# A recommendation tower: all pair dots of a tile in one piece, with layers 1 and 2 in another shape, layer 3 on VectorE and the table lookups in another order

## The chip, the cores and the metric

The kernel runs on one core of a Trainium2 chip. The metric is the time on the device in microseconds (us), as a median of runs; lower is better.

## The reference, cut to what matters

For each of 2048 rows of a batch, 27 embedding rows of 128 floats are looked up, one in each of 27 tables, by integer ids. The dot products of all 351 pairs of the 27 rows follow, 16 dense values are appended, and three dense layers end in one number for each row.

```python
e = jnp.stack([tbl_f[ids[:, f]] for f in range(27)], axis=1)   # (2048, 27, 128)
dot = jnp.einsum('bnd,bmd->bnm', e, e)                         # all pairs
z = flat[:, idx]                                               # the 351 pairs i < j
h = jnp.concatenate([z, dense_ctx], axis=1)                    # (2048, 367)
h = jnp.maximum(h @ W_top1 + b_top1, 0.0)                      # (2048, 512)
h = jnp.maximum(h @ W_top2 + b_top2, 0.0)                      # (2048, 256)
y = h @ W_top3                                                 # (2048, 1)
```

## The kernel before, in words

**Tiles.** The batch is cut into 16 tiles of 128 rows. Two neighbouring tiles make a half (`HT = 2`, 8 halves of 256 rows). Everything is float32.

**Two ways to look up.** 17 features are gathered (`GATHERED`): GpSimd issues one indirect DMA for each feature and tile (L298), 272 in all, into `emb`, which holds two tiles; a slot is free again once TensorE has turned the rows of two tiles ago. TensorE transposes them four features at a time, a "quad" (L331; five quads to a tile, the last with one feature), and ScalarE copies each quad into `embT` (L488). The ten smallest tables (`ONE_HOT`, seven of 1000 rows and three of 1250) stay in SBUF, split into two parts. VectorE compares the broadcast ids of a half with row numbers and so builds one-hot matrices (L426), one for each chunk of 125 table rows, 8 or 10 chunks to a table; TensorE multiplies both parts of the chunk with it, 256 columns wide (L321); ScalarE copies the result (L481). One such step for a half and a table is a "hot" step, 80 in all. The one-hot matrices live in `SLOTS` = 6 groups of two chunks, and VectorE builds one table ahead (`LOOK = 1`). SyncE loads the ids of a table `IDS` tables ahead (L247), in its queue behind the tables and the weights.

**Dots.** For each batch row TensorE multiplies the 27 columns of `embT` with themselves (L347), 128 such products to a tile. They come as 256 pairs of a weight load and a matmul of 27 columns each, so 512 instructions to a tile. The four 32-partition strips of `gram_ps` take four rows at a time. VectorE then transposes the result into `flat` (L442, L443) and ScalarE copies each pair once into `pairs` (L496, the step "ring").

**Layers.** "flat" turns `pairs` (three transposes, L359) and copies them to `flatT` (L500). Layer 1 is 12 matmuls, 128 wide (24 matmul instructions, L370), then a ReLU on ScalarE (L505); layer 2 is 8 matmuls (16 instructions, L380), then bias and ReLU in two halves (L513); layer 3 is 2 matmuls with a single weight column (4 instructions, L387) and a copy (L521).

**Order.** `plan(t)` writes the steps of tile t down by hand (L93 to L125) and `ORDER` is run through in the same order by TensorE, ScalarE and VectorE. After `START`, with the ten hot steps of half 0 between the quads of tile 0, come four hot steps of half 1. From then on an odd tile t carries: its five quads; the dots of tile t-1 in four pieces of 8 groups (64 instruction pairs), one behind each of the first four quads; flat, layer 1, layer 2 and layer 3 of tile t-2, one behind each of these pieces; and the last six hot steps of the next half. An even tile has its dots in three pieces (80, 88 and 88 pairs) with nothing but a quad and a layer between them, and all its four hot steps at its end. The dots of a tile wait for its last quad and for the last hot step of its own half; in the order before, that step is over a whole tile earlier. SyncE stores two tiles of results at a time from one partition (L236).

Of the kernel before, what the change touches and what calls it, by code (L numbers as in the profile page):

```python
# [43 lines left out]
def dlrm_tower(nc, dense, idx_rows, ids_hot, tables, w1, w2, b2, w3, y):  # L44
# [4 lines left out]
    C2 = w3.shape[1]  # L49
    H2 = C2 * P  # L50
# [15 lines left out]
    PITCH = 28  # L66
# [7 lines left out]
    IDS = 7  # L74
# [6 lines left out]
    YB = 2  # L81
# [10 lines left out]

    def plan(t):  # L93
        h, odd = divmod(t, HT)
        last = t == T - 1
        hots = []
        if h + 1 < HALVES:
            first = O * 2 // 5
            hots = [("hot", h + 1, o) for o in (range(first, O) if odd else range(first))]
        parts = 2 if last else 4 if odd else 3  # L100
        dots = []
        if t > 0:
            cuts = [GROUPS32 * i // parts for i in range(parts + 1)]
            dots = [("dots", t - 1, a, b) for a, b in zip(cuts, cuts[1:])]
        rest = [(kind, t - 2) for kind in ("flat", "layer1", "layer2", "layer3")] if t > 1 else []
        held = 0 if odd else QUADS - 2
        out = []
        for q in range(QUADS):
            if t > 0:
                out.append(("quad", t, q))  # L110
            out += dots[q:q + 1]
            if last and q == 1:
                out += rest[1:]
            elif last and q == 2:
                out += [("ring", t - 1), ("flat", t - 1)]
            elif last and q == 3:
                out += [(kind, t - 1) for kind in ("layer1", "layer2", "layer3")]
            elif not last or q == 0:
                out += rest[q:q + 1]
            if q >= held:  # L120
                a, b = q - held, QUADS - held
                out += hots[len(hots) * a // b:len(hots) * (a + 1) // b]
        if t > 0 and not last:
            out.append(("ring", t - 1))
        return out  # L125

    HOT0 = [("hot", 0, o) for o in range(O)]
    START = []
    for q in range(QUADS):
        START += HOT0[O * q // QUADS:O * (q + 1) // QUADS] + [("quad", 0, q)]  # L130
    END = [("dots", T - 1, 0, GROUPS32), ("ring", T - 1)]
    END += [(kind, T - 1) for kind in ("flat", "layer1", "layer2", "layer3")]
    ORDER = START + [step for t in range(T) for step in plan(t)] + END

# [10 lines left out]
    with ctx:  # L145
# [20 lines left out]
        flatT = sb("flatT", [P, 2, KC, TILE])  # L166
        h1T = sb("h1T", [P, C1, TILE])
        h2T = sb("h2T", [P, C2, TILE])
        y_sb = sb("y_sb", [1, 2, YB * TILE])
        w1_sb = sb("w1_sb", [P, KC, H1])  # L170
        w2_sb = sb("w2_sb", [P, C1, H2])
        w3_sb = sb("w3_sb", [P, C2])
        b2_sb = sb("b2_sb", [P, C2])
# [13 lines left out]
        out_ps = ps("out_ps", [P, 512])  # L187
# [18 lines left out]
        staged = [sem(f"staged{o}") for o in range(O)]  # L206
        high_ready = sem("high_ready")
# [19 lines left out]
        y_summed = sem("y_summed")  # L227
        y_ready = sem("y_ready")
        y_stored = [sem(f"y_stored{b}") for b in range(2)]
# [4 lines left out]
        def store(sp, b):  # L234
            sp.wait_ge(y_ready, YB * (b + 1))
            sp.dma_start(y[b * YB * TILE:(b + 1) * YB * TILE, :].rearrange("n a -> a n"),  # L236
                         y_sb[0:1, b % 2, :]).then_inc(y_stored[b % 2], 16)

        @block.sync
        def _(sp):  # L240
# [24 lines left out]
            sp.dma_start(w3_sb[:, :], w3).then_inc(weights_loaded, 16)  # L265
            sp.dma_start(b2_sb[:, :], b2).then_inc(weights_loaded, 16)  # L266
            stored = 0
            for n in range(O, len(HOTS)):

                if HOTS[n][1] - 1 >= stored + 3:  # L270
                    store(sp, stored)
                    stored += 1
                load_ids(n)
            for b in range(stored, T // YB):
                store(sp, b)
            for b in range(2):
                sp.wait_ge(y_stored[b], 16 * (T // YB // 2))

# [25 lines left out]
        def _(pe):  # L304
# [57 lines left out]
            def layer1(t):  # L362
                pe.wait_ge(flatT_ready, t + 1)
                if t == 0:
                    pe.wait_ge(weights_loaded, WEIGHTS)
                else:
                    pe.wait_ge(h1_ready, t)
                for c in range(C1):
                    for k in range(KC):
                        mm = pe.matmul(h1_ps[:, c * TILE:(c + 1) * TILE], w1_sb[0:KR, k, c * P:(c + 1) * P],  # L370
                                       flatT[0:KR, t % 2, k, :], start=(k == 0), stop=(k == KC - 1))
                mm.then_inc(h1_summed, 1)

            def layer2(t):
                pe.wait_ge(h1_ready, t + 1)
                if t > 0:
                    pe.wait_ge(y_ready, t)
                for c in range(C2):
                    for k in range(C1):
                        mm = pe.matmul(out_ps[:, c * TILE:(c + 1) * TILE], w2_sb[:, k, c * P:(c + 1) * P],  # L380
                                       h1T[:, k, :], start=(k == 0), stop=(k == C1 - 1))
                mm.then_inc(h2_summed, 1)

            def layer3(t):
                pe.wait_ge(h2_ready, C2 * (t + 1))
                for k in range(C2):
# [188 lines left out]
```

## Time and profile before

| | |
|---|---|
| median of 3 runs | 405.42 us (403.98 to 406.58) |
| the profiled execution | 406.24 us, of which the span from first to last instruction is 404.4 us |
| TensorE (PE) matmuls busy | 362.8 us, 90% |
| TensorE weight loads (PEld) | 331.7 us, 82% |
| VectorE (DVE) | 253.3 us, 63% |
| ScalarE (ACT) | 170.9 us, 42% |
| GpSimd (POOL) | 260.9 us, 65% |
| mean granted TensorE clock | 0.975 of full |

The profile is one execution. "Idle before" is the time that an engine stood still ahead of a group of instructions, with what released it; "issue" there means that nothing in the profile shows what it waited for. SPq is SyncE's queue. Matmuls overlap in the pipeline, so the time that one group costs is read from its start to the start of the next one.

### The profile page before, as it was taken

How to read it: one execution, taken by the hardware profiler on the slowest of the kernel's cores; microseconds unless marked ns; L12 is line 12 of the kernel's file. 1: busy time of each engine (PE TensorE's matmuls, PEld its weight loads, DVE VectorE, ACT ScalarE, POOL GpSimd, SP SyncE). 2: the span in 40 equal slices, each digit the busy share in tenths (PEclk: the TensorE clock that was granted, in tenths of full speed). 3: DMA queues.
4: the chain of work that ended last, by engine and by line, in shares of the span. 5: the costliest groups of instructions: out<-in, count | busy, mean ns of one | idle time of the engine just before them, and what ended most of it. 6: DMA issues, size and time to landing. Idle time of an engine off the chain costs nothing.

```text
span 404.4 us, 14846 instructions
## 1 busy us (share of the span) xinstructions
PE 362.8 (90%) x6496; PEld 331.7 (82%) x6496; DVE 253.3 (63%) x751; ACT 170.9 (42%) x267; POOL 260.9 (65%) x280
## 2 busy tenths in 40 slices
PE   1887699999998999999998999999998999986846
PEld 1766599889997999989997999899988999865745
DVE  4999799939665684929583866749492966311010
ACT  3455325354534354354334454535334454463311
POOL 6777777777777777777777777777777777100000
PEclk9998989999999999999999999999999999999877
DMA  6999985343333242323433243324333322000000
GB/s 184 234 239 228 220 133 120 82 86 89 88 76 94 61 106 73 89 72 95 93 79 88 69 107 77 89 61 107 81 83 78 80 55 55 23 3 3 0 3 0
DMA packets 23233, 36.44 MB, mean 90 GB/s; under 512 B 6425, under 2 KB 17441, under 8 KB 23169
## 3 DMA queue, kind: packets, MB, share of 16 engines
q1 hardware_dynamic: 14464, 17.66, 18.9%
q0 software_dynamic: 8704, 17.84, 18.8%
q8 instruction: 51, 0.84, 0.8%
q14 instruction: 14, 0.11, 0.1%
HBM read 35.47 MB, written 0.01 MB: 88 GB/s over the span
## 4 chain that ended last, share of the span: by engine, by line
PE 79%; DMA 5%; ACT 4%; DVE 4%; issue 4%; SPq 3%; DVEq 0%; ACTq 0%
PE embT_ps L321 39%; PE h_ps L370 12%; PE gram_ps L347 11%; PE out_ps L380 8%; PE embT_ps L331 5%; DMA ids<-in_ids_hot 4%; DVE one_hot L426 3%; PE flat_ps L359 2%; PE out_ps L387 2%; SPq L265 2%; ACT pairs L496 1%; ACT h2T L513 1%; DVE tbl L412 1%; DMA embT<-in_tbl 1%; SPq L266 1%
## 5 line engine op out<-in xcount | busy, mean ns | idle before, releaser
L298 POOL DMA_INDIRECT emb<-in_tbl,idx x272 | 260.0, 956 | 84.2 <-issue 81.5
L426 DVE TENSOR_SCALAR one_hot<-ids,row_of 125x256 fp32r<-125x256 int32 x688 | 214.8, 386 | 43.2 <-PE embT_ps L321 40.5
L321 PE MATMUL embT_ps<-one_hot,tbl 125*128 125x256 f32 x1376 | 192.4, 294 | 19.0 <-DVE one_hot L426 18.8
L321 PEld LDWEIGHTS embT_ps<-one_hot,tbl 125*128 125x128 f32 x1376 | 175.9, 195 | 31.2 <-issue 15.9
L481 ACT COPY embT<-embT_ps 128x256 f32<-128x256 f32 x80 | 53.0, 662 | 131.0 <-PE embT_ps L321 131.0
L488 ACT COPY embT<-embT_ps 128x512 f32<-128x512 f32 (+1 forms) x80 | 81.9, 1024 | 0.6 <-PE embT_ps L331 0.5
L442 DVE STREAM_TRANSPOSE flat<-gram_ps 128x864 f32<-128x864 f32 x16 | 17.3, 1083 | 87.9 <-PE gram_ps L347 87.9
L347 PEld LDWEIGHTS gram_ps<-embT 128*27 128x27 f32 x4096 | 42.7, 104 | 18.0 <-issue 14.9
L347 PE MATMUL gram_ps<-embT 128*27 128x27 f32 x4096 | 50.8, 193 | 6.8 <-issue 5.7
L370 PE MATMUL h_ps<-flatT,w_sb 126*128 126x128 f32 x384 | 51.2, 294 | 1.9 <-issue 1.1
L370 PEld LDWEIGHTS h_ps<-flatT,w_sb 126*128 126x128 f32 x384 | 48.1, 206 | 3.1 <-ACT flatT L500 1.3
L331 PE MATMUL embT_ps<-ident,emb 128*128 128x128 f32 x272 | 43.3, 275 | 0.0
L380 PE MATMUL out_ps<-h1T,w_sb 128*128 128x128 f32 x256 | 32.9, 282 | 2.1 <-ACT h1T L505 2.1
L331 PEld LDWEIGHTS embT_ps<-ident,emb 128*128 128x128 f32 x272 | 32.4, 142 | 0.7 <-issue 0.7
L380 PEld LDWEIGHTS out_ps<-h1T,w_sb 128*128 128x128 f32 x256 | 29.8, 191 | 3.2 <-ACT h1T L505 2.7
L505 ACT ACTIVATE h1T<-h_ps 128x512 f32<-128x512 f32 x16 | 9.6, 599 | 50.6 <-PE h_ps L370 50.6
L513 ACT ACTIVATE h2T<-out_ps,b_sb 128x128 f32<-128x128 f32 x32 | 10.0, 364 | 28.2 <-PE out_ps L380 28.2
L412 DVE TENSOR_TENSOR tbl<-embT,tbl 125x1024 fp32r<-125x1024 f32 (+1 forms) x10 | 13.3, 1327 | 5.3 <-ACT tbl L469 5.3
L496 ACT COPY pairs<-flat 128x351 f32<-128x351 f32 x16 | 13.3, 830 | 6.3 <-DVE flat L443 6.3
L469 ACT CAST tbl<-embT 125x1024 fp32r<-125x1024 f32 (+1 forms) x10 | 11.2, 1115 | 10.7 <-DMA embT<-in_tbl 10.7
L359 PE MATMUL flat_ps<-ident,pairs 128*126 128x128 f32 x48 | 9.1, 300 | 5.9 <-ACT pairs L496 5.3
L387 PE MATMUL out_ps<-h2T,w_sb 128*1 128x128 f32 x64 | 9.6, 271 | 4.1 <-ACT h2T L513 4.1
(18 smaller groups left out, 37.9 us busy)
## 6 DMA issues: line engine op xcount, KB each, us to landing
ids<-in_ids_hot SPq DMA_DIRECT2D x80, 128.0 KB
emb<-in_tbl,idx POOLq DMA_INDIRECT x272
embT<-in_tbl SPq DMA_DIRECT2D x7, 448.0 KB
embT<-in_tbl SPq DMA_DIRECT2D x3, 560.0 KB
w_sb<-in_W_ring SPq DMA_DIRECT2D x1, 756.0 KB
w_sb<-in_W_top SPq DMA_DIRECT2D x1, 512.0 KB
embT<-in_tbl SPq DMA_DIRECT2D x7, 52.0 KB
idx<-in_idx_rows SPq DMA_DIRECT2D x1, 202.5 KB, 7.9
```

What stands on the lines that cost most here:

```text
L298: pool.indirect_dma_start(emb[:, t % EB, s, :], None, tables[f][:, :], bass.IndirectOffsetOnAxis(ap=idx[:, t, f:f + 1], axis=0),).then_inc ...
L321: mm = pe.matmul(out[:, 0:HN], tbl[0:ROWS, part, AT[o] + chunk, :], one_hot[0:ROWS, k % SLOTS, c, :], start=(chunk == 0 and part == 0), st ...
L331: mm = pe.transpose(out[:, i * P:(i + 1) * P], emb[:, t % EB, s, :], ident[:, :])
L347: mm = pe.matmul(gram_ps[32 * j:32 * j + FEATS, b, at * FEATS:(at + 1) * FEATS], rows, rows, start=True, stop=True)
L370: mm = pe.matmul(h1_ps[:, c * TILE:(c + 1) * TILE], w1_sb[0:KR, k, c * P:(c + 1) * P], flatT[0:KR, t % 2, k, :], start=(k == 0), stop=(k = ...
L380: mm = pe.matmul(out_ps[:, c * TILE:(c + 1) * TILE], w2_sb[:, k, c * P:(c + 1) * P], h1T[:, k, :], start=(k == 0), stop=(k == C1 - 1))
L387: mm = pe.matmul(out_ps[0:1, C2 * TILE:(C2 + 1) * TILE], w3_sb[:, k:k + 1], h2T[:, k, :], start=(k == 0), stop=(k == C2 - 1))
L412: dve.tensor_tensor(tbl[0:ROWS, 1, AT[o]:AT[o + 1], :], raw(o, 0, ROWS).rearrange("p (c d) -> p c d", d=D), tbl[0:ROWS, 0, AT[o]:AT[o + 1] ...
L426: done = dve.tensor_scalar(one_hot[0:ROWS, k % SLOTS, c, :], ids[0:ROWS, n % IDS, :], row_of[0:ROWS, KINDS.index(CH[o]), chunk:chunk + 1], ...
L481: act.copy(embT_feats[:, at:at + HT, GF + o, :], embT_ps[USE["hot", h, o] % BANKS][:, 0:HN].rearrange("p (t c) -> p t c", t=HT),).then_inc ...
L488: act.copy(embT_feats[:, t % TB, quad(q)[0]:quad(q)[0] + n, :], embT_ps[USE["quad", t, q] % BANKS][:, 0:n * P].rearrange("p (f c) -> p f c ...
L496: act.copy(pairs[:, t % 2, :, 1:HALF + 1], ring()).then_inc(pairs_ready, 1)
```

## The change

- The dots of tile t-1 stand in one piece behind the first quad of tile t (`cuts = [0, GROUPS32]`).
- The hot steps are spread evenly: five in each tile, one behind each quad. Half h is looked up in the tiles 2h-1 and 2h, so its last hot step is the last step but one ahead of the first quad of tile 2h+1, behind which the dots of tile 2h stand. The four hot steps of half 1 ahead of tile 1 are gone from there.
- Layer 1 runs for two tiles at once, 256 columns wide, in two calls of 6 matmuls in the odd tiles; layer 2 swaps its operands (`h1T` is the weight, `w2` moves with 256 columns), 4 matmuls to a tile, two tiles in the even tiles. The last two tiles run layer 1 alone.
- Layer 3 leaves TensorE and ScalarE: VectorE adds the bias (from PSUM) and then multiplies, clamps and sums in one instruction. `w3` and `b2` are broadcast over the partitions when loaded, and each tile's result is stored by itself, a number to a partition.
- For half 0 ScalarE turns the ids into floats before VectorE reads them. `PITCH`, the row pitch of `embT`, goes from 28 to 27 floats, `IDS` from 7 to 6.

```diff
-    PITCH = 28
+    PITCH = FEATS
-    IDS = 7
+    IDS = 6
     def plan(t):
-        h, odd = divmod(t, HT)
+        h, odd = divmod(t + 1, HT)
+        odd = 1 - odd
...
+        if t == 0:
+            hots = HOT0
+        elif h < HALVES:
+            hots = [("hot", h, o) for o in (range(O // 2) if odd else range(O // 2, O))]
+        cuts = [0, GROUPS32]
+        dots = [("dots", t - 1, a, b) for a, b in zip(cuts, cuts[1:])] if t > 0 else []
+        after = [[] for _ in range(QUADS)]
+        if t > 1:
+            after[0].append(("flat", t - 2))
+        if t > 2 and odd:
+            after[1].append(("layer1", t - 3))
+            after[2].append(("layer1", t - 2))
+        elif t > 2:
+            after[1].append(("layer2", t - 4))
+            after[2].append(("layer2", t - 3))
+        if t == T - 1:
+            after[3] += [("layer2", t - 3), ("ring", t - 1), ("flat", t - 1), ("layer2", t - 2)]
         out = []
         for q in range(QUADS):
+            mine = hots[len(hots) * q // QUADS:len(hots) * (q + 1) // QUADS]
+            if t == 0:
+                out += mine
+            out.append(("quad", t, q))
+            out += dots[q:q + 1]
+            out += after[q]
             if t > 0:
+                out += mine
+        if 0 < t < T - 1:
             out.append(("ring", t - 1))
...
+    END = [("dots", T - 1, 0, GROUPS32), ("layer1", T - 2), ("ring", T - 1), ("flat", T - 1), ("layer2", T - 2),
+           ("layer1", T - 1), ("layer2", T - 1)]
...
+            def layer1(n):
+                alone = n >= T - HT
...
+                width = TILE if alone else HT * TILE
+                first, count = (0, C1) if alone else (n % HT * C1 // HT, C1 // HT)
+                for i in range(count):
+                    c = first + i
                     for k in range(KC):
+                        mm = pe.matmul(h1_ps[:, i * width:(i + 1) * width], w1_sb[0:KR, k, c * P:(c + 1) * P],
+                                       x[:, k, :], start=(k == 0), stop=(k == KC - 1))
...
+                for k in range(C1):
+                    mm = pe.matmul(h2_ps[:, :], h1T[:, k, t % HT * TILE:(t % HT + 1) * TILE], w2_sb[:, k, :],
+                                   start=(k == 0), stop=(k == C1 - 1))
...
+            def layer3(t):
+                dve.wait_ge(h2_summed, t + 1)
...
+                dve.tensor_tensor(h2[:, :], h2_ps[:, :], b2_sb[:, :], ALU.add).then_inc(h2_ready, 1)
+                dve.wait_ge(h2_ready, t + 1)
+                dve.scalar_tensor_tensor(h2[:, :], h2[:, :], 0.0, w3_sb[:, :], ALU.max, ALU.mult,
+                                         accum_out=y_sb[:, t:t + 1]).then_inc(y_ready, 1)
...
+            def float_ids(n):
+                act.wait_ge(ids_loaded[n % IDS], 16 * (n // IDS + 1))
+                act.copy(ids[0:ROWS, n % IDS, :].bitcast(F32), ids[0:ROWS, n % IDS, :]).then_inc(ids_as_floats, 1)
```

## Rows read from the trace of the kernel before

**Rows 1.** The page: TensorE clock and DMA rate in 40 equal slices; the chain by line.

```profile
PEclk9998989999999999999999999999999999999877
...
GB/s 184 234 239 228 220 133 120 82 86 89 88 76 94 61 106 73 89 72 95 93 79 88 69 107 77 89 61 107 81 83 78 80 55 55 23 3 3 0 3 0
...
PE embT_ps L321 39%; PE h_ps L370 12%; PE gram_ps L347 11%; PE out_ps L380 8%; PE embT_ps L331 5%; DMA ids<-in_ids_hot 4%; DVE one_hot L426 3%; PE flat_ps L359 2%; PE out_ps L387 2%; SPq L265 2%; ACT pairs L496 1%; ACT h2T L513 1%; DVE tbl L412 1%; DMA embT<-in_tbl 1%; SPq L266 1%
```

**Rows 2.** Groups of TensorE from 99.6 to 358.7 us, the tiles 3 to 14.

```profile
L347 PE MATMUL gram_ps<-embT 128*27 128x27 f32 x3072 | 38.8, 192 | 2.5 <-issue 2.1
...
L387 PE MATMUL out_ps<-h2T,w_sb 128*1 128x128 f32 x48 | 7.2, 271 | 1.7 <-ACT h2T L513 1.7
```

**Rows 3.** Timeline of TensorE in tile 7: start us, us, what.

```profile
194.34 2.94 PE L370 MATMUL h_ps<-flatT,w_sb 126*128 126x128 f32 x24
197.04 2.17 PE L321 MATMUL embT_ps<-one_hot,tbl 125*128 125x256 f32 x16
199.04 0.60 PE L331 MATMUL embT_ps<-ident,emb 128*128 128x128 f32 x4
199.58 0.74 PE L347 MATMUL gram_ps<-embT 128*27 128x27 f32 x64
200.25 2.05 PE L380 MATMUL out_ps<-h1T,w_sb 128*128 128x128 f32 x16
202.06 2.16 PE L321 MATMUL embT_ps<-one_hot,tbl 125*128 125x256 f32 x16
```

**Rows 4.** Timeline of TensorE: the second of three pieces of dots in tile 8.

```profile
216.29 1.09 PE L347 MATMUL gram_ps<-embT 128*27 128x27 f32 x76
218.42 0.30 PE L347 MATMUL gram_ps<-embT 128*27 128x27 f32 x12 [1.04 <-issue]
```

**Rows 5.** Timeline of TensorE in tile 15 and behind it.

```profile
358.77 0.77 PE L331 MATMUL embT_ps<-ident,emb 128*128 128x128 f32 x5
...
363.86 0.93 PE L347 MATMUL gram_ps<-embT 128*27 128x27 f32 x87 [1.62 <-issue]
...
375.15 4.55 PE L370 MATMUL h_ps<-flatT,w_sb 126*128 126x128 f32 x24
...
384.49 1.80 PE L347 MATMUL gram_ps<-embT 128*27 128x27 f32 x193 [0.48 <-ACT embT L488]
388.28 0.78 PE L347 MATMUL gram_ps<-embT 128*27 128x27 f32 x63 [1.99 <-issue]
...
393.01 5.49 PE L370 MATMUL h_ps<-flatT,w_sb 126*128 126x128 f32 x24 [0.57 <-ACT flatT L500]
```

**Rows 6.** Stretches: from:to, length, busy of PE, PEld, DVE, ACT, POOL, granted clock, DMA.

```profile
361.70:365.10 3.40, 1.78 (x132) 1.65 (x132) 0.27 (x1) 1.21 (x2) 0.00 (x0) 1.00 0.03 5
...
385.60:389.00 3.40, 1.41 (x146) 1.23 (x133) 0.00 (x0) 0.00 (x0) 0.00 (x0) 0.97 0.02 5
389.00:399.20 10.20, 6.46 (x32) 5.70 (x28) 1.64 (x3) 1.86 (x3) 0.00 (x0) 0.51 0.01 2
```

**Rows 7.** DMA queues: TensorE's instructions as they are fetched (packets, MB).

```profile
q8 instruction: 51, 0.84, 0.8%
```

**Rows 8.** Timeline of the start: TensorE and VectorE around the first ids of half 1.

```profile
47.77 0.27 PE L331 MATMUL embT_ps<-ident,emb 128*128 128x128 f32 x1
...
49.83 12.35 DVE L426 TENSOR_SCALAR one_hot<-ids,row_of 125x256 fp32r<-125x256 int32 x40 [2.69 <-DMA ids<-in_ids_hot]
```

**Rows 9.** Timeline: TensorE at tile 3, then ScalarE, VectorE and GpSimd in the loop.

```profile
99.60 0.60 PE L331 MATMUL embT_ps<-ident,emb 128*128 128x128 f32 x4
...
278.37 0.66 ACT L481 COPY embT<-embT_ps 128x256 f32<-128x256 f32 x1 [1.24 <-PE embT_ps L321]
...
205.38 1.08 DVE L442 STREAM_TRANSPOSE flat<-gram_ps 128x864 f32<-128x864 f32 x1 [0.70 <-PE gram_ps L347]
...
206.97 8.70 DVE L426 TENSOR_SCALAR one_hot<-ids,row_of 125x256 fp32r<-125x256 int32 x28
...
344.95 0.94 POOL L298 DMA_INDIRECT emb<-in_tbl,idx  x1 [0.31 <-issue]
```

More of the change, by code:

```diff
@@ L48, in dlrm_tower @@
     KR, KC, H1 = w1.shape
-    C2 = w3.shape[1]
-    H2 = C2 * P
+    H2 = w2.shape[1]
     C1 = H1 // P
@@ L93, in plan @@
     def plan(t):
-        h, odd = divmod(t, HT)
-        last = t == T - 1
+        h, odd = divmod(t + 1, HT)
+        odd = 1 - odd
         hots = []
[L97 to L104, printed above, removed]
@@ L105, in plan @@
-        rest = [(kind, t - 2) for kind in ("flat", "layer1", "layer2", "layer3")] if t > 1 else []
-        held = 0 if odd else QUADS - 2
+        if t == 0:
[7 more added lines that the diff above has]
+            after[0].append(("flat", t - 2))
@@ L112, in plan @@
[L112 to L122, printed above, removed]
@@ L127, in dlrm_tower @@
     HOT0 = [("hot", 0, o) for o in range(O)]
[L128 to L133, printed above, removed]
+    END = [("dots", T - 1, 0, GROUPS32), ("layer1", T - 2), ("ring", T - 1), ("flat", T - 1), ("layer2", T - 2),
+           ("layer1", T - 1), ("layer2", T - 1)]
+    ORDER = [step for t in range(T) for step in plan(t)] + END
     USE = {step: u for u, step in enumerate(step for step in ORDER if step[0] in ("quad", "hot"))}
@@ L226, in dlrm_tower, with halves_of, store @@
         h2_ready = sem("h2_ready")
-        y_summed = sem("y_summed")
         y_ready = sem("y_ready")
-        y_stored = [sem(f"y_stored{b}") for b in range(2)]
+        y_stored = sem("y_stored")
         WEIGHTS = 16 * 4
         block = ctx.enter_context(nc.Block())
[L234 to L237, printed above, removed]
+        def halves_of(t):
+            return t if t >= T - HT else t // HT * HT + HT - 1
+        def store(sp, t):
+            sp.wait_ge(y_ready, t + 1)
+            sp.dma_start(y[t * TILE:(t + 1) * TILE, :], y_sb[:, t:t + 1]).then_inc(y_stored, 16)
         @block.sync
@@ L273, in _ @@
                 load_ids(n)
[L274 to L277, printed above, removed]
+            for t in range(stored, T):
+                store(sp, t)
+            sp.wait_ge(y_stored, 16 * T)
         @block.gpsimd
@@ L376, in layer2 @@
                 if t > 0:
[L377 to L381, printed above, removed]
-                mm.then_inc(h2_summed, 1)
-            def layer3(t):
-                pe.wait_ge(h2_ready, C2 * (t + 1))
-                for k in range(C2):
-                    mm = pe.matmul(out_ps[0:1, C2 * TILE:(C2 + 1) * TILE], w3_sb[:, k:k + 1], h2T[:, k, :],
-                                   start=(k == 0), stop=(k == C2 - 1))
-                mm.then_inc(y_summed, 1)
+                    pe.wait_ge(h2_ready, t)
@@ L418, in build @@
                 _, _, o = HOTS[n]
-                dve.wait_ge(ids_loaded[n % IDS], 16 * (n // IDS + 1))
+                of = ids[0:ROWS, n % IDS, :]
+                if n < O:
+                    dve.wait_ge(ids_as_floats, n + 1)
+                    of = of.bitcast(F32)
+                else:
+                    dve.wait_ge(ids_loaded[n % IDS], 16 * (n // IDS + 1))
                 for i in range(GROUPS[o]):
@@ L425, in build @@
                         chunk = i * GROUP + c
-                        done = dve.tensor_scalar(one_hot[0:ROWS, k % SLOTS, c, :], ids[0:ROWS, n % IDS, :],
+                        done = dve.tensor_scalar(one_hot[0:ROWS, k % SLOTS, c, :], of,
                                                  row_of[0:ROWS, KINDS.index(CH[o]), chunk:chunk + 1], None,
@@ L528, in _ @@
                     split_high(ahead)
+                    float_ids(ahead)
                     ahead += 1
```

83 lines of the change are left out of this document (35 added, 48 removed).

## The prediction, made before the changed kernel was run

> **What bounds the kernel now.** The chain of waits comes first: nearly 80% of it is TensorE work, half of that the one-hot products of L321 [rows 1]. TensorE bounds the kernel, and between tile 3 and tile 15 it hardly stands still. So a step is priced by what it takes from TensorE, start to start. In tile 7 [rows 3]: layer 1 takes 197.04 - 194.34 = 2.70 us (24 instructions, 112 ns each); a hot step of 8 chunks 2.00 us, or 0.25 us a chunk; a quad 0.54; 64 pairs of the dots 0.67 (10.5 ns a pair); layer 2 1.81. VectorE needs 8.70 / 28 = 0.311 us for a chunk and 1.59 us for the two transposes and the dense columns behind the dots [rows 9]. GpSimd issues its last gather at 344.95 us [rows 9], nearly 40 us ahead of the last quad, so it stays off the path unless TensorE gains more than that.
>
> The second view is where TensorE waits for "issue". It does so inside long runs of dots and nowhere else in the loop: 1.04 us behind 76 pairs in tile 8 [rows 4], 1.62 us in tile 15, and 1.99 us in the one place where 256 pairs already stand in one piece, behind the loop [rows 5]. There 193 pairs run for 1.80 us, TensorE idles 1.99, and 63 more take 0.78: 4.57 us for work that at 10.5 ns a pair takes 2.7. The queue that brings TensorE's instructions moved 0.84 MB in 51 packets [rows 7]; 6496 weight loads and as many matmuls are 12992 instructions, so a packet holds about 255 of them, 128 pairs. My reading, an estimate: dots eat a packet in 1.3 us, the next is asked for when the one before it is begun, and it is usable 3.1 to 3.7 us later. 3.4 - 1.3 = 2.1 us of standstill for each piece of 256 pairs. Of the Trainium skill, "Runtime: NRT & Kernel Launch", section "Instruction fetch mechanics", says the opposite: the fetch is hidden, because dispatch is slower than the refill. The trace disagrees, with 1.99 us. By the page there would be no standstill; that is a rival below.
>
> The third view is the clock. It is full through the loop [rows 1]. Behind the burst with 1.62 us of idle it stayed full (361.7 to 365.1 us, 1.00); behind the one with 1.99 us it fell to its lower level, 1.2 GHz: 389.0 to 399.2 us at 0.51 [rows 6], where layer 1 took 5.49 us instead of 2.9 [rows 5].
>
> **The parts, against the span of 404.4 us.** The profiled execution took 406.24 us, 1.84 more than its span and 0.8 more than the median.
>
> *To quad (3,0), before at 99.60 us [rows 9].* The last quad of tile 0 starts at 47.77 us, and the first ids of half 1 let VectorE build on at 49.83, after 2.69 us of idle [rows 8]. Now a quad and dots stand there, and the wait is covered. `w3` and `b2` as broadcasts put 0.26 MB ahead of these ids, about 1.1 us at the 220 to 239 GB/s of those slices [rows 1]; that is covered too, all but some 1 us where VectorE's transposes queue behind the late build. Floats instead of integers could speed up VectorE's first 86 chunks, but the tables' landing paces them as well: 0, bounds -1.5 and +1. So quad (1,0) at 48.0; tile 1 costs 0.54 + 4.7 (dots) + 10.0 (five hot steps) + 1.7 (the other 13 transposes) + 1 = 17.9; tile 2 costs 0.54 + 4.7 + 0.4 (flat) + 11.5 (46 chunks) + 1.7 + 0.35 = 19.2. That ends at 85.1, 14.5 us earlier, but four hot steps (8.0 us) and the layers of tile 0 are still to do.
>
> *Tiles 3 to 14, before 259.2 us (99.60 to 358.77) [rows 9, 5].* Plus 8.0 for the four hot steps. Dots: 12 pieces of 4.7 us against 38.8 + 2.5 us [rows 2]: +15.1. Layer 3: 7.2 + 1.7 us go, less the overlap of its matmuls' ends: -8.2 [rows 2]. Layer 1 has half the instructions, each twice as wide; no row has the shape. It could cost no more than a narrow one (112 ns, a gain of 2.7 us a pair of tiles) or twice as much; since a 27-column pair takes 10.5 ns and a 128-column instruction 112, columns count, and I take twice. The same for layer 2, 8 x 0.224 = 1.79 against 1.81. Both: -1. The flat transposes no longer wait for the ring: -1.1. The dots of even tiles now wait for the copy of the hot step just ahead (0.66 us [rows 9], of which a quad hides most): 6 x 0.35 = +2.1. VectorE's order matters, since it waits for the dots and for each layer 2 before it builds on: behind dots it has one table in stock (2.0 us of TensorE) plus flat and a quad (0.94), and needs 1.59 + 0.62 for the next group; its two instructions for layer 3 have no row, 0.3 to 0.5 us each by the 0.311 of a chunk, and in 22 us it has some 6 idle. I take 0. ScalarE's added and removed work, single-tile stores and `IDS` 6 lie beside other work: 0; if ids came late, VectorE would starve. `PITCH` 27: 0, bounds 10% of the dots each way, 4 us. Sum: 259.2 + 8.0 + 15.1 - 8.2 - 1 - 1.1 + 2.1 = 274.1, so quad (15,0) at 359.2, level with before.
>
> *Tail, before 45.6 us.* Now, in order: quad and wait 0.9, dots 4.7, flat 0.4, three quads 1.6, two double layer 1 calls 5.4, two layer 2 3.6, flat 0.4, waits for ReLUs 0.5, last quad 0.13 and its copy 0.6, dots 4.6, layer 1 of tile 14 2.7 (which hides transposes and ring), flat 0.4, layer 2 1.8, layer 1 2.7, ReLU 0.7, layer 2 1.8, VectorE 0.9, store 1.6: 35.4, or 10 less. It saves the lone waits of four small layers and the low clock in layer 1 (4.55 and 5.49 us [rows 5]). End 394.6.
>
> *Where packets end.* A tile has about 775 instructions, three packets and a few, so the ends of packets drift slowly through the dots. Near their head or tail a second standstill comes. By my count this meets tiles 12 to 15; bounds 1 and 8 us, taken 4. 398.6.
>
> *The clock.* Every piece now has the idle behind which the clock fell once. The fall depends on where the idle lies, so I take it for 7 of 16 pieces. A short low stretch costs 4.55 - 2.9 = 1.7 us [rows 5], so 12 us: span 410.6, time 412.4, and by the median 411.6.
>
> **Rivals.**
> *A, the clock holds.* The standstill is below what matters, as at 1.62 us. Decides if it stays near 1.8 us. Place: behind each piece of dots; price 12 us less. Time 399.6, faster. For it: one burst with 1.62 us, full clock. Against: 1.99 us and a fall, on the same form. Chance 0.22, give or take 5 us.
> *B, short standstills.* The fetch is asked for earlier in the loop than behind it, and costs 1.0 us as in tile 8: 16 x 1.1 less and no falls, no second ones: about 378; up to 391 in between. Against it: tile 8 reached 1.04 us with a quad and a flat between. Chance 0.14.
> *C, no standstill.* 34 us less than the 394.6, but gathers end at 346 and the rest of the tail takes 22: 368 to 370. The Trainium skill's "Runtime: NRT & Kernel Launch" would have it so. The rows contradict it: 0.03.
> *D, long falls.* Each fall lasts 10 us as behind the loop, with 5 us lost: 398.6 + 36 + 1 = 435. For it, the one row there is; against, layer 1 at 375.15 ran low for one stretch only. Chance 0.11.
>
> **How the numbers follow.** My forecast has 0.50, its own range 405 to 421 (4 to 10 falls, packets, pitch). The 8-in-10 range leaves out D, C and the better half of B: 389 to 422. A measurement of this kernel tells 1% from no change, so faster means below 401.4 and slower above 409.5. Faster: B, C and 0.13 of A, 0.30. Within: 0.09 of A and 0.15 of the forecast, 0.24. Slower: 0.46.
>
> **What will show it.** In the changed profile: in each tile one group of about 185 to 200 pairs of L347, an idle of 1.9 to 2.2 us put down to "issue", then the rest; L347's idle sum near 32 us. The granted clock below full in slices of the loop, with hot steps of 4 us instead of 2.0. Quad (3,0) near 85 us, quad (15,0) between 359 and 372. The gap in front of the dots of even tiles near 0.35 us, no VectorE waits above it. L370 with half the instructions at 220 ns. I am wrong if the dots run through, if VectorE starves TensorE behind them, or if the wide matmuls cost as little as narrow ones (-20 us).

## The result: slower by 9.5%, outside the range

| | before | changed |
|---|---|---|
| median of 4 runs each, on one chip | 404.82 us (403.98 to 406.58) | 443.68 us (441.0 to 446.71) |
| ratio | | 1.0953 (95%: 1.0897 to 1.1009) |
| the profiled execution | 406.24 us, span 404.4 | 444.45 us, span 441.3 |
| mean granted clock | 0.975 | 0.921 |

Slower had the largest chance, but the time lies 21.7 us above the upper end of the range. On another chip the changed kernel took 437.65 us against 407.79, a ratio of 1.0743. So its price is 30 to 39 us.

The page of the changed kernel, against [rows 1]: busy time by engine, the clock in 40 slices, the DMA queue that SyncE's transfers are in (packets, MB, share of 16 engines), and the chain by engine.

```profile
span 441.3 us, 14146 instructions
PE 361.4 (82%) x6136; PEld 333.0 (75%) x6136; DVE 261.5 (59%) x799; ACT 167.6 (38%) x229; POOL 264.9 (60%) x280
...
PEclk9999869998989898999889896999969998997987
...
q1 hardware_dynamic: 16752, 17.92, 17.3%
...
PE 75%; issue 12%; DMA 7%; ACT 3%; DVE 1%; POOL 1%; SPq 0%; ACTq 0%; DVEq 0%
```

TensorE has 5% fewer instructions and is busy for as long as before. What grew is the time in which it waits for nothing that the profile shows: "issue" is 12% of the chain, 53 us (4% before). And the clock is now below full in slices all through the loop.

The groups of TensorE in tiles 3 to 14 (93.25 to 391.4 us), against [rows 2]:

```profile
L346 PE MATMUL gram_ps<-embT 128*27 128x27 f32 x3072 | 50.6, 205 | 32.4 <-issue 26.9 <-ACT embT L499 2.2
...
L375 PE MATMUL h_ps<-flatT,w_sb 126*128 126x256 f32 x144 | 33.1, 379 | 0.0
L384 PE MATMUL h_ps<-w_sb,h1T 128*128 128x256 f32 x96 | 22.7, 379 | 0.0
```

The dots cost 50.6 + 32.4 = 83.0 us in twelve tiles, 6.9 a piece, where 4.7 were forecast and 3.4 was the price before.

Two kinds of pieces make this up. They are named by the tile in whose steps they stand (it is the dots of the tile before). First the timeline of TensorE in tile 11, which stands for the odd tiles:

```profile
292.24 1.98 PE L346 MATMUL gram_ps<-embT 128*27 128x27 f32 x146 [0.38 <-ACT embT L499]
296.18 1.76 PE L346 MATMUL gram_ps<-embT 128*27 128x27 f32 x110 [1.96 <-issue]
```

That is the forecast's picture: one standstill of 1.96 us in the middle, where by the forecast's count a packet of instructions ends. In the tiles 3, 4, 5, 7, 9, 11 and 13 it comes after 186, 183, 176, 166, 156, 146 and 136 pairs: the end of the packet drifts by ten pairs in two tiles. Now tile 10, which stands for the tiles 6, 8, 10, 12 and 14, and SyncE's queue just ahead of it:

```profile
264.40 1.08 PE L346 MATMUL gram_ps<-embT 128*27 128x27 f32 x78
268.15 0.23 PE L346 MATMUL gram_ps<-embT 128*27 128x27 f32 x2 [2.67 <-issue]
268.97 0.18 PE L346 MATMUL gram_ps<-embT 128*27 128x27 f32 x1 [0.60 <-issue]
...
270.21 3.77 PE L346 MATMUL gram_ps<-embT 128*27 128x27 f32 x174 [0.42 <-issue]
```

```profile
259.80 0.91 SPq L237 DMA_DIRECT2D out_y<-y_sb  x2
```

TensorE stops after 78 pairs, then does a pair or two at a time with 0.4 to 0.6 us between them, then runs on at the lower clock: 9.5 us for a piece. Some 5.5 us before the stop SyncE issued two stores of `y`. It issues one at 160.24 us, two at 208.80, 259.80 and 311.20 and three at 361.77, and the dots stop at 165.6, 214.5, 265.5, 316.5 and 367.5, after 60 to 93 pairs. That is ahead of the place where a packet ends in the tiles beside them (176 to 136 pairs). The pieces of the tiles 6, 8, 10, 12 and 14 take 9.23, 8.52, 9.52, 8.77 and 7.11 us, those of the odd tiles between them 4.8 to 5.7. Each store writes 128 single numbers from 128 partitions: the queue q1 has 16752 packets where a kernel with a single store at the end (below) has 14480, 142 more for each of the 16.

Stretches of the changed kernel (from:to, length, busy of PE, PEld, DVE, ACT, POOL, granted clock, DMA), behind the dots of tile 10 and of tile 11 and over the loop:

```profile
264.00:269.00 5.00, 1.71 (x86) 1.40 (x84) 0.42 (x2) 2.33 (x3) 3.78 (x5) 1.00 0.83 58
269.10:275.80 6.70, 5.58 (x185) 4.93 (x185) 1.77 (x4) 0.48 (x1) 2.57 (x3) 0.50 0.28 75
...
296.40:299.70 3.30, 3.30 (x116) 3.17 (x103) 1.72 (x4) 0.48 (x1) 2.01 (x3) 0.50 0.18 46
...
64.00:391.00 327.00, 291.48 (x5030) 271.88 (x5029) 208.40 (x664) 129.57 (x176) 216.85 (x226) 0.93 0.37 73
```

Behind a stop the granted clock is 0.50, that is 1.2 GHz. Over the loop it is 0.93, so TensorE is at 1.2 GHz for some 14% of 327 us, 45 us in ten stretches, and loses up to 22 us by it.

### The profile page after: what moved, and what is told of

Same layout as the page of the kernel before. It is cut to its first block, busy times and chain, and to the rows that moved or that the text cites. A ratio compares the mean times of both kernels' runs of the same rounds, so it can differ in the third digit from the quotient of the medians.

```text
span 441.3 us, 14146 instructions
## 1 busy us (share of the span) xinstructions
PE 361.4 (82%) x6136; PEld 333.0 (75%) x6136; DVE 261.5 (59%) x799; ACT 167.6 (38%) x229; POOL 264.9 (60%) x280
## 3 DMA queue, kind: packets, MB, share of 16 engines
q1 hardware_dynamic: 16752, 17.92, 17.3%
## 4 chain that ended last, share of the span: by engine, by line
PE 75%; issue 12%; DMA 7%; ACT 3%; DVE 1%; POOL 1%; SPq 0%; ACTq 0%; DVEq 0%
PE embT_ps L320 36%; PE gram_ps L346 14%; PE h_ps L375 10%; PE h_ps L384 6%; PE embT_ps L330 6%; DMA embT<-in_tbl 4%; PE flat_ps L358 2%; DMA emb<-in_tbl,idx 2%; ACT embT L499 1%; POOL emb L297 1%; DVE one_hot L426 1%; ACT tbl L483 0%; ACT embT L506 0%; DMA idx<-in_idx_rows 0%; DVE tbl L407 0%
## 5 line engine op out<-in xcount | busy, mean ns | idle before, releaser
L426 DVE TENSOR_SCALAR one_hot<-ids,row_of 125x256 fp32r<-125x256 int32 (+1 forms) x688 | 210.5, 380 | 30.2 <-PE embT_ps L320 24.9
L320 PE MATMUL embT_ps<-one_hot,tbl 125*128 125x256 f32 x1376 | 202.1, 303 | 19.7 <-DVE one_hot L426 18.0
L320 PEld LDWEIGHTS embT_ps<-one_hot,tbl 125*128 125x128 f32 x1376 | 185.6, 203 | 25.9 <-issue 15.4
L346 PE MATMUL gram_ps<-embT 128*27 128x27 f32 x4096 | 64.0, 204 | 47.9 <-issue 40.8
L346 PEld LDWEIGHTS gram_ps<-embT 128*27 128x27 f32 x4096 | 52.5, 115 | 60.8 <-issue 52.6
L375 PE MATMUL h_ps<-flatT,w_sb 126*128 126x256 f32 (+1 forms) x216 | 46.5, 369 | 0.3 <-ACT h1T L528 0.3
L375 PEld LDWEIGHTS h_ps<-flatT,w_sb 126*128 126x128 f32 x216 | 38.2, 202 | 4.6 <-issue 0.5
L518 ACT COPY flatT<-flat_ps 126x384 f32<-126x384 f32 x16 | 7.7, 480 | 79.4 <-PE flat_ps L358 79.4
L384 PE MATMUL h_ps<-w_sb,h1T 128*128 128x256 f32 x128 | 30.6, 382 | 1.2 <-ACT h1T L524 0.7
L384 PEld LDWEIGHTS h_ps<-w_sb,h1T 128*128 128x128 f32 x128 | 23.1, 190 | 4.3 <-ACT h1T L524 0.9
L528 ACT ACTIVATE h1T<-h_ps 128x512 f32<-128x512 f32 x14 | 8.4, 598 | 19.5 <-PE h_ps L375 19.5
L483 ACT CAST tbl<-embT 125x1024 fp32r<-125x1024 f32 (+1 forms) x10 | 11.3, 1132 | 10.7 <-DMA embT<-in_tbl 10.7
```

The source lines that it names most:

```text
L320: mm = pe.matmul(out[:, 0:HN], tbl[0:ROWS, part, AT[o] + chunk, :], one_hot[0:ROWS, k % SLOTS, c, :], start=(chunk == 0 and part == 0), st ...
L346: mm = pe.matmul(gram_ps[32 * j:32 * j + FEATS, b, at * FEATS:(at + 1) * FEATS], rows, rows, start=True, stop=True)
L375: mm = pe.matmul(h1_ps[:, i * width:(i + 1) * width], w1_sb[0:KR, k, c * P:(c + 1) * P], x[:, k, :], start=(k == 0), stop=(k == KC - 1))
L384: mm = pe.matmul(h2_ps[:, :], h1T[:, k, t % HT * TILE:(t % HT + 1) * TILE], w2_sb[:, k, :], start=(k == 0), stop=(k == C1 - 1))
L426: done = dve.tensor_scalar(one_hot[0:ROWS, k % SLOTS, c, :], of, row_of[0:ROWS, KINDS.index(CH[o]), chunk:chunk + 1], None, ALU.is_equal)
```

## The experiments

The theory on record, **packets**: a piece of 256 pairs eats instructions faster than they are fetched, and the standstills let the clock fall. Its rival, found in the timeline, **stores**: the stores of single numbers slow the supply of instructions down when dots stand behind them, and so make longer standstills and more falls.

### Each alone and both

*Four pieces.* The dots of a tile in four pieces of 64 pairs, one behind each quad:

```diff
-        cuts = [0, GROUPS32]
+        cuts = [GROUPS32 * i // 4 for i in range(5)]
```

> The changed kernel with the dots of a tile in four pieces again, one behind each of the first four quads; all else stays. Theory: the loss is the one piece, that is the standstills of TensorE inside it and the clock falls behind them. Then the dots of a tile cost 3.0 to 3.4 us instead of the 6.7 us measured in tiles 3 to 14, the clock stays full in the loop, and the time falls to 370 to 392 us, under the kernel before. Rival: the new table order or the layers cost as much as the one piece, VectorE starving TensorE; then it stays above 410 us with DVE waits on L320.

*One store.* All results are kept, turned by TensorE at the end and stored by one DMA of 16 rows:

```diff
-                while HT * HOTS[n][1] - 1 >= stored + 7:
-                    store(sp, stored)
-                    stored += 1
                 load_ids(n)
-            for t in range(stored, T):
-                store(sp, t)
-            sp.wait_ge(y_stored, 16 * T)
+            sp.wait_ge(y_copied, 1)
+            sp.dma_start(y.rearrange("(t p) a -> t (p a)", p=TILE), y_rows[:, :]).then_inc(y_stored, 16)
+            sp.wait_ge(y_stored, 16)
...
+            pe.wait_ge(y_ready, T)
+            pe.transpose(flat_ps[0:T, 0:P], y_sb[:, :], ident[:, :]).then_inc(y_turned, 1)
```

> The changed kernel, dots in one piece, but the results are kept in SBUF, turned once at the end and stored by one DMA of 16 rows, in place of 16 stores of 128 single numbers. Theory S: these stores disturb TensorE's instruction supply; the standstills of 7 to 9.5 us in tiles 6, 8, 10, 12 and 14 go, each of these blocks takes about 5 us like the odd ones, and the time falls by 18 to 25 us to 418 to 426 us. Rival P: they come from where the instruction packets end in the dots; then the blocks stay at 7 to 9.5 us and the time stays within 4 us of 443.7.

*Both edits.*

> Both of the above: four pieces and one store. Theory S: a little below the kernel with four pieces alone, by 2 to 10 us, since its supply is disturbed less: 365 to 385 us. Rival P: the same as with four pieces alone, within 2 us.

*The kernel before, its dots in one piece*, without anything else of the change:

```diff
-        parts = 2 if last else 4 if odd else 3
+        parts = 1
```

> The kernel before with one thing changed: the dots of a tile in one piece behind its first quad. It has no small stores. My mechanism (a standstill of 1.1 to 2.3 us in each piece, then a clock fall behind most of them): dots 5.0 us a tile instead of 3.4, plus 8 to 12 low stretches of 1.7 us, so 425 to 445 us. Rival: the piece costs little where hot steps follow densely and the clock holds: 405 to 415 us.

The kernel before took 407.42 us beside them. The upper left number is the changed kernel's, from other chips. Of the four runs of one piece with one store, one took 402.95 us at a mean clock of 0.979 and three took 409.6 to 410.2 at 0.958 to 0.967, so it has no ratio:

| | 16 small stores | one store |
|---|---|---|
| one piece | 443.7 (437.7 on a third chip) | 409.71 (402.95 to 410.24) |
| four pieces | 402.98, ratio 0.9851 (0.981 to 0.9892) | 387.92, ratio 0.9541 (0.9491 to 0.959) |

The kernel before in one piece: 437.08 us, ratio 1.0765 (1.0713 to 1.0817), so 29.7 us more than with its pieces. Of the four expectations only this one was met. The two kernels with four pieces came out slower than expected, and one store in one piece faster.

Groups of dots over the whole run of these kernels, the first of four pieces, the second of one store (a run of 409.83 us), the third of both, the fourth of the kernel before in one piece:

```profile
L346 PE MATMUL gram_ps<-embT 128*27 128x27 f32 x4096 | 56.7, 193 | 10.5 <-issue 5.6 <-ACT embT L499 2.6 <-ACT embT L506 1.0
```

```profile
L341 PE MATMUL gram_ps<-embT 128*27 128x27 f32 x4096 | 54.5, 199 | 34.6 <-issue 27.6 <-ACT embT L496 2.6 <-ACT embT L503 1.0
```

```profile
L341 PE MATMUL gram_ps<-embT 128*27 128x27 f32 x4096 | 55.9, 193 | 7.0 <-issue 2.8 <-ACT embT L496 2.6 <-ACT embT L503 1.0
```

```profile
L347 PE MATMUL gram_ps<-embT 128*27 128x27 f32 x4096 | 54.0, 194 | 29.5 <-issue 25.0 <-ACT embT L488 0.5
```

Both causes are there, and they feed each other. A piece of 256 pairs stands still for 27.6 / 16 = 1.7 us and 25.0 / 16 = 1.6 us on average in the two kernels that have no small stores (single pieces 0.6 to 3.1 us); with four pieces 2.8 us are left in all. In the table, one piece costs 15.0 to 21.8 us with one store (by the run of 402.95 or by the median) and 35 to 41 with sixteen; sixteen stores cost 15.1 us with four pieces and 28 to 41 with one. With one piece and sixteen stores part of the width comes from comparing chips.

The stretches of the loop show the clock's part: one store with one piece, then with four (columns as above).

```profile
64.00:368.00 304.00, 276.51 (x4982) 258.86 (x4980) 205.29 (x647) 125.43 (x172) 212.96 (x224) 0.96 0.31 78
```

```profile
61.00:363.00 302.00, 295.75 (x5304) 266.30 (x5303) 210.56 (x656) 131.39 (x183) 215.79 (x228) 1.00 0.31 79
```

At 0.96 the loss is some 0.04 x 304 = 12 us, at 1.00 it is none. The last column but one is the DMA engines' busy share, 0.31 with one store. With sixteen it is 0.39 from 64 to 364 us, and the queues say where the rise lies (packets, MB, share of 16 engines): first the changed kernel, then one piece with one store, both from 64 to 364 us.

```profile
q0 software_dynamic: 7081, 14.53, 26.3%
q1 hardware_dynamic: 10224, 8.25, 11.2%
```

```profile
q0 software_dynamic: 7221, 14.80, 20.1%
q1 hardware_dynamic: 8830, 8.04, 10.2%
```

q1 holds the small stores, q0 GpSimd's gathers. The stores' own queue rises by one point only. The gathers rise by six, with fewer packets (27.9% against 19.6% with four pieces). So the small stores take little time of the engines themselves; it is the packets of another queue that take longer while the stores are under way. The instructions come as packets too, in q8. Here are the same queues of the changed kernel for 6 us each: from 264 us, with the stop of tile 10, and from 290.5 us, with the dots of tile 11.

```profile
q0 software_dynamic: 99, 0.20, 65.5%
...
q8 instruction: 1, 0.02, 3.9%
```

```profile
q0 software_dynamic: 157, 0.33, 21.8%
...
q8 instruction: 1, 0.02, 1.0%
```

3.9% of 16 engines over 6 us are 3.7 us for one packet of instructions, 1.0% are 1.0 us. The trace has each such packet with its start and length. Those of the tiles 10, 12 and 14 took 3.74, 3.30 and 2.49 us; those of the tiles 6 and 8 took 0.93 and 0.97 but started 3.8 and 4.6 us behind the first dots, against 0.95 to 2.1 us in the other tiles from 2 to 13. So in the five tiles with stores just ahead the packet had landed 3.2 to 5.6 us behind the first dots, in the others 2.0 to 3.1. With one store, in one piece, none took over 1.6 us in the whole run, though in tile 4 the packet landed 4.1 us behind the first dots and the piece idled 2.65. That the instructions come late behind small stores is shown by this; why the stores hold other packets up, and why TensorE stops ahead of the end of a packet, is not.

### A chip on which nothing could be told

Four kernels ran twice on a chip on which the kernel before itself took 678 us. Their granted clock was 0.79 to 0.82, and in the first of them TensorE idled for "issue" in the table steps too (23.7 us). The first is the changed kernel with its stores moved in SyncE's queue, to the ids of another table:

```diff
-                while HT * HOTS[n][1] - 1 >= stored + 7:
+                while HOTS[n][2] == 2 and HT * HOTS[n][1] - 1 >= stored + 7:
```

> Again the changed kernel with only the moment of the loop's small stores moved to just behind the dots of the even tiles, since on the chip of the run before the kernel before itself took 678 us. Theory S: the blocks of 7 to 9.5 us in the tiles 6, 8, 10 and 12 fall to 5 to 6 us; the time falls by 10 to 16 us against 443.7, so 1.05 to 1.07 times the kernel before. Rival, number of stores or SyncE's waits: 1.085 to 1.10 times.

The second has one store and the dots in two pieces, `cuts = [0, GROUPS32 // 2, GROUPS32]`:

> Again the kernel with one store and the dots in two pieces of 128 pairs. Packet theory: a packet of instructions is 128 pairs long, so the standstill in a piece is 0 to 0.7 us and the clock holds: 0.95 to 0.97 times the kernel before. Rival, each piece stands still by itself: 0.985 to 1.01 times.

The third is the kernel before in one piece, with sixteen stores of 128 numbers each in place of its eight stores of rows (the numbers stored are taken from `dense_sb`, so `y` is left out):

> Again the kernel before with dots in one piece (1.077 times the kernel before) and its 8 row stores replaced by 16 stores of 128 single numbers taken from the dense values (the output is not the result). Theory S: blocks of 7 us and more where a store comes shortly ahead of the dots; 1.09 to 1.13 times. Rival, small stores harmless here: 1.07 to 1.085 times.

The fourth has one store and multiplies only every second group of pairs, so half of the dots is left out:

> Again the kernel with one store and one piece, with every second group of the dots left out (128 pairs a tile, half of the dot products missing). Packet theory: no standstill over 0.5 us in most tiles, full clock in the loop, 365 to 385 us where the kernel before takes 405. Rival, the standstill belongs to the step: 1.5 us or more in most tiles.

| | first time | second time |
|---|---|---|
| kernel before | 678.13 | 679.11 |
| stores moved | 586.33 | 589.23, ratio 0.8654 (0.8553 to 0.8754) |
| two pieces, one store | 631.91 | 632.86, ratio 0.9286 |
| before, one piece, small stores | 626.98 | 618.28, ratio 0.9041 |
| half the dots (one run each) | 539.23 | 538.16 |

The dots of the kernel with its stores moved idled 110.4 us on that chip, 98.7 of it for "issue"; on a normal chip they idle 47.5 in all. Here the kernel with one piece beats the kernel before by 13% and two pieces by 7%, another order than on the normal chips. What slows this chip wasn't found, and these runs decide nothing about the theories. Half the dots never ran on a normal chip, so of short pieces only those of the kernel with two pieces were measured there.

### The same on a normal chip

The kernel before took 407.79 us here. First the changed kernel itself again:

> The changed kernel itself, unaltered, beside the three below on the same chip: 1.09 to 1.10 times the kernel before where that takes 405 us; where it takes 678 us, Theory S makes it slower than with the stores moved (0.865 times), the rival within 1% of that.

437.65 us, ratio 1.0743 (1.0651 to 1.0836), below the expected 1.09. Then with its stores moved (the edit above):

> The changed kernel with only the moment of the loop's small stores moved to just behind the dots of the even tiles. Theory S: the blocks of 7 to 9.5 us in the tiles 6, 8, 10, 12 fall to 5 to 6 us, 10 to 16 us less than the changed kernel beside it. Rival, number of stores or SyncE's waits: within 4 us of it.

438.88 us, ratio 1.0763 (1.0686 to 1.084): no gain, which is the rival's number. The timeline says why: a store in SyncE's queue, and TensorE around it.

```profile
259.71 1.77 SPq L237 DMA_DIRECT2D out_y<-y_sb  x2
```

```profile
259.18 2.34 PE L346 MATMUL gram_ps<-embT 128*27 128x27 f32 x153
...
265.83 0.25 PE L346 MATMUL gram_ps<-embT 128*27 128x27 f32 x3 [1.79 <-issue]
```

SyncE runs some steps ahead, and the stores went out during the dots instead of just ahead of them. The stop with single pairs behind it came later in the piece, after 249 pairs here, but it came. My expectation had put the stores in the wrong place.

The kernel before with one piece and small stores:

> The kernel before with dots in one piece (1.077 times the kernel before) and 16 stores of 128 single numbers, taken from the dense values, in place of 8 row stores (the output is not the result). Theory S: blocks of 7 us and more where a store comes shortly ahead of the dots, 1.09 to 1.13 times the kernel before. Rival, small stores harmless here: 1.07 to 1.085 times.

470.85 us, ratio 1.1567 (1.1483 to 1.165): 33.8 us more than in one piece with its own stores (437.08, on another chip). But for the one piece, nothing of the change is in this kernel. Its SyncE queue, its TensorE behind a store, and its dots over the whole run:

```profile
254.89 0.91 SPq L237 DMA_DIRECT2D out_y<-dense_sb  x2
```

```profile
258.38 1.11 PE L349 MATMUL gram_ps<-embT 128*27 128x27 f32 x104
263.74 0.54 PE L349 MATMUL gram_ps<-embT 128*27 128x27 f32 x2 [4.25 <-issue]
```

```profile
L349 PE MATMUL gram_ps<-embT 128*27 128x27 f32 x4096 | 60.0, 199 | 47.3 <-issue 42.3 <-ACT embT L490 0.5
```

The same stop, 4.25 us long, 4.6 us behind the store, then single pairs. "Issue" went from 25.0 to 42.3 us. So the small stores alone do it, in another order of steps and other layers, and for more than the expected 1.13. The moment isn't what differs: with its own stores of rows the same kernel issues five of them 3.4 to 3.6 us ahead of a piece, and these pieces take 4.6 to 5.8 us without single pairs. With small stores at the same distance they take 8.1 to 10.7. The form of the stores and their number (16 for 8) changed together, and no run tells these two apart.

Two pieces and one store:

> The kernel with one store and the dots in two pieces of 128 pairs. Packet theory: a packet of instructions is 128 pairs long, so the standstill in a piece is 0 to 0.7 us and the clock holds: 0.95 to 0.97 times the kernel before. Rival, each piece stands still by itself: 0.985 to 1.01 times.

390.34 us, ratio 0.9563 (0.9491 to 0.9636), about as much as four pieces. Its dots idle 7.4 us for "issue" in all.

A piece of 128 pairs, one packet, mostly runs through (25 of 30 in this run; the other five idle 0.3 to 1.6 us), and the clock doesn't fall from 65.7 to 373 us. That fits a piece being harmless as long as it is no longer than the instructions that lie ready; how many lie ready, no row says.

### Stores amid the table steps, and the best kernel

The stores moved again, by `HOTS[n][2] == 3`, so that they go out in the table steps, some 10 us behind the start of the dots in even tiles:

> The changed kernel (1.074 to 1.095 times the kernel before) with the loop's small stores moved once more: with two loads of ids they had gone out during the dots of the even tiles, now they go out some 10 us behind their start, 13 us ahead of the next dots. Theory S (a small store disturbs TensorE's instruction supply 3.4 to 9 us after it is issued): all blocks in the loop 5 to 6.5 us, 1.03 to 1.05 times the kernel before. Rival, the number of small stores counts and not their moment: 1.07 times or more.

431.01 us, ratio 1.0587 (1.0489 to 1.0684) beside 407.5 of the kernel before: between the two expectations, and its interval overlaps that of the unaltered changed kernel (1.0651 to 1.0836). So the time hardly decides, but the timeline does. TensorE's dots in tile 10, a store behind them, and the stretch behind the store:

```profile
255.06 2.60 PE L346 MATMUL gram_ps<-embT 128*27 128x27 f32 x153
258.88 1.47 PE L346 MATMUL gram_ps<-embT 128*27 128x27 f32 x103 [1.22 <-issue]
```

```profile
265.23 0.92 SPq L237 DMA_DIRECT2D out_y<-y_sb  x2
```

```profile
264.00:269.00 5.00, 5.00 (x35) 4.69 (x34) 4.64 (x17) 2.22 (x3) 3.85 (x4) 1.00 0.72 72
```

The DMA engines are nearly as busy as behind the store of the changed kernel (0.72, against 0.83 there), but TensorE runs through, 5.00 of 5.00 us: a table step takes 35 matmuls in that time, where dots would take over 200. The pieces of the tiles 2 to 13 take 4.3 to 6.7 us, none with single pairs. Yet the time is only 6.6 us less than on the chip above: three of the later stores go out together at 341.84 us, just ahead of tile 14, and two more around the last dots at 394.65. The piece in tile 14 takes 8.5 us and the last one 9.2.

At last the best parts together. Four pieces, one store, and the dots of the last tile in two pieces with layer 1 of tile 14 between them (the first two edits, and this):

```diff
-    END = [("dots", T - 1, 0, GROUPS32), ("layer1", T - 2), ("ring", T - 1), ("flat", T - 1), ("layer2", T - 2),
-           ("layer1", T - 1), ("layer2", T - 1)]
+    END = [("dots", T - 1, 0, GROUPS32 // 2), ("layer1", T - 2), ("dots", T - 1, GROUPS32 // 2, GROUPS32),
+           ("layer2", T - 2), ("ring", T - 1), ("flat", T - 1), ("layer1", T - 1), ("layer2", T - 1)]
```

> The kernel with four pieces and one store (0.954 times the kernel before), and the last tile's dots, which still stood in one piece at the end (5.4 us with a standstill of 2.8), in two pieces with layer 1 of tile 14 between and layer 2 of tile 14 behind. Packet theory: the standstill goes, 1 us of ring and transposes is exposed instead, 1 to 3 us less: 0.945 to 0.952. Rival: the exposed ring takes it all back: 0.953 to 0.957.

385.31 us (383.4 to 388.23), ratio 0.9486 (0.9433 to 0.9539). It beats both kernels. Its clock, its dots, and the timeline of the last ones:

```profile
PEclk9899989999999999999999999999999999999999
...
L341 PE MATMUL gram_ps<-embT 128*27 128x27 f32 x4096 | 54.5, 192 | 4.1 <-ACT embT L496 2.6 <-ACT embT L503 1.0
...
365.26 1.27 PE L341 MATMUL gram_ps<-embT 128*27 128x27 f32 x128 [0.50 <-ACT embT L503]
366.46 2.94 PE L370 MATMUL h_ps<-flatT,w_sb 126*128 126x128 f32 x24
369.33 1.27 PE L341 MATMUL gram_ps<-embT 128*27 128x27 f32 x128
```

With layer 1 between them, both pieces of 128 pairs run through; in the kernel with four pieces and one store, whose last dots are one piece, this place held a standstill of 2.61 us. No idle of the dots is put down to "issue" any more. Against four pieces and one store it is 2.6 us less, by the ratios to the kernel before 0.9486 and 0.9541, whose intervals overlap.

## Why the prediction was wrong

**The step that failed:** "ScalarE's added and removed work, single-tile stores and `IDS` 6 lie beside other work: 0". I counted the bytes and the issues of the stores, and nothing for what they do to other packets. Only SyncE waits for a store, at the very end, but it goes over the same DMA engines that bring TensorE's instructions, and these packets landed late behind it. Sixteen small stores cost 28 to 41 us in one piece. Without them (one store) the kernel took 403 to 410 us against a forecast of 411.6 for the whole change.

Not all of the miss in the span (441.3 - 410.6 = 30.7) is theirs. Against the profiled run with one store (408.0) the changed kernel is 33.3 us longer: 5.3 of it lies ahead of quad (3,0), where no store has gone out yet (the first does at 160.24 us), 18.3 in the tiles 3 to 14, and 9.7 in the tail, of which 5.5 is the wait for the last store. And that the kernel with one store meets the forecast so well is in part luck: the wide matmuls cost less than forecast, the clock fell more often (both below).

**What bounds it** was right: TensorE start to start. That TensorE waits for "issue" nowhere in the loop but inside dots was not quite so: in the tiles 3 to 14 of the kernel before, 1.1 us of it stand in front of layer 1 and 0.6 in front of flat, beside 2.1 in dots. Against the sum without clock and packet ends, the start is 7.7 us longer, tiles 3 to 14 are 24.1, the tail 14.9: 46.7 in all, of which 16 had been allowed for.

*To quad (3,0)*: forecast 85.1, measured 92.80. The first piece of dots stands while tables, weights and ids still load, and its standstill is 5.52 us instead of 2.1 (3.70 in the other profile of the same kernel):

```profile
51.09 2.23 PE L346 MATMUL gram_ps<-embT 128*27 128x27 f32 x150 [0.15 <-ACT embT L506]
58.84 1.58 PE L346 MATMUL gram_ps<-embT 128*27 128x27 f32 x106 [5.52 <-issue]
...
92.80 0.60 PE L330 MATMUL embT_ps<-ident,emb 128*128 128x128 f32 x4
```

*Dots, one standstill of 2.1 us a piece*: right in kind, place and drift, slightly too long (1.6 to 1.7 us on average without small stores). Of the second standstills, counted for the tiles 12 to 15, one came: in tile 15, 1.74 us. The one piece as a cause is shown by undoing the one piece and by doing it alone: the kernel before lost 29.7 us by it, and by the forecast's terms one piece without the rest was worth 15.1 + 12 + 4 = 31. With small stores the pieces of tiles 3 to 14 cost 83.0 us against 56.4.

*The clock*: "7 of 16 pieces (12 us)". Measured: a fall behind 13 of the 16 pieces with the small stores and up to 22 us in the loop, behind 10 of 16 with one store (some 12 us in its loop). The falls came behind the stops in mid-piece, and also behind plain ones: in tile 11, behind 1.96 us, it was 0.50 from 296.40 to 299.70 us. The length of the idle alone doesn't decide: the three pieces without a fall idled 1.10, 0.92 and 1.45 us, while one with 1.22 had a fall behind it.

*Layers*: wide matmuls "taken twice" as long as narrow ones (224 ns). The timeline in tile 7:

```profile
199.02 2.75 PE L375 MATMUL h_ps<-flatT,w_sb 126*128 126x256 f32 x12
201.42 2.27 PE L320 MATMUL embT_ps<-one_hot,tbl 125*128 125x256 f32 x16
```

12 in 2.40 us are 200 ns each, and layer 2 took 192. So they cost 144 x 0.024 + 96 x 0.032 = 6.5 us less than forecast. Layer 3 on VectorE, 0.42 us for each of its two instructions, lies in the forecast 0.3 to 0.5, and VectorE starved nobody in the loop (the hot steps idle 1.6 us in twelve tiles). The wait for the copy of the hot step ahead, forecast 0.35 us, is 0.38 in front of the dots of tile 10 (the row in tile 11 above). The flat transposes no longer wait. So the change without its one piece and its small stores is worth 19.5 us (407.42 to 387.92), which these two turned into a loss.

*Tail*: forecast 35.4, measured 50.3 us (391.02 to 441.3). The last dots stand still for 3.42 us, the clock is low in layer 1, and the last store is waited for:

```profile
391.02 0.60 PE L330 MATMUL embT_ps<-ident,emb 128*128 128x128 f32 x4
...
413.73 1.79 PE L346 MATMUL gram_ps<-embT 128*27 128x27 f32 x190 [0.50 <-ACT embT L506]
418.94 0.90 PE L346 MATMUL gram_ps<-embT 128*27 128x27 f32 x66 [3.42 <-issue]
419.76 4.30 PE L375 MATMUL h_ps<-flatT,w_sb 126*128 126x128 f32 x24
```

The list of waits has that last one for SyncE, in the changed kernel and in the one before (us, times, longest):

```profile
SPq L142 <- DMA out_y<-y_sb: 6.6, 1, 6.6
```

```profile
SPq L277 <- DMA out_y<-y_sb: 0.9, 1, 0.9
```

6.6 us where 1.6 were forecast: that is what a store of 128 single numbers costs when it is waited for. One store of 16 rows was waited for 1.1 us.

**The rivals.** A (the clock holds), B (short standstills) and C (none) fell: the clock was at 0.50 behind standstills, these took 1.6 us or more a piece on average, and 25 to 28 us of "issue" stood in the kernels with one piece and without small stores. D had a price near the result, 435, but by long falls; seven of the ten low stretches in the loop were of 3.4 us and three of 6.8, and it wasn't D's mechanism that brought the time there. No rival had the stores.

## What to carry to other kernels

Don't price a store by its bytes: sixteen stores with one number to a partition cost 15 to 41 us here, because other queues' packets, those with instructions too, come late behind them. Turn such results first and store rows. Keep a run of short matmuls short (128 pairs were mostly harmless here, 256 never), with slower work between two such runs, since the standstill costs twice, once itself and once by the clock behind it. And where an engine idles for "issue", look at what every DMA queue did in the 6 us before.

## What the runs showed of the hardware

- A store of 128 numbers of 4 bytes was waited for 6.6 us at the end, one of 16 rows 1.1 us, one of a single row 0.9.
- With ten such small stores in 300 us the share of the gathers' packets in the time of the DMA engines rose from 20.1% to 26.3%, and that of the queue with the stores from 10.2% to 11.2%. A packet of instructions behind them took up to 3.74 us instead of some 1.0.
- Behind such a store TensorE ran one or two pairs at a time, with 0.4 to 0.6 us between them, after a stop of 2.67 or 4.25 us. Of the Trainium skill, "Runtime: NRT & Kernel Launch", section "Instruction fetch mechanics", calls the crossing of a block mostly hidden; in these runs it cost 0.6 to 5.5 us in a piece of 256 pairs, while the table steps of twelve tiles idled 1.6 us for "issue" in all.
- A matmul with 256 columns took 192 to 200 ns, less than two of 128 columns at 112 ns.
- One chip ran the kernel before in 678 us instead of 405 to 408, at a mean granted clock of 0.79 to 0.81, and put the kernels in another order.
